# A fused attention and mixture-of-experts layer: all attention products in four column tiles, and four pieces of work moved by a step or a unit

## What is computed

```python
logits = jnp.einsum('bhnd,bhmd->bhnm', Q, K) * scale        # Q, K rotated
logits = jnp.where(causal, logits, -jnp.inf)
attn = einsum('bhnm,bhmd->bhnd', softmax(logits), V) @ Wo.T
x = layernorm(x + attn)
xf = layernorm(x, ln_w, ln_b)
router = xf @ router_w;  top = argmax(router);  score = sigmoid(max(router))
shared = (silu(xf @ sh_gate) * (xf @ sh_up)) @ sh_down
xe = xf * score of its own expert e
routed = (silu(xe @ gate_w[e]) * (xe @ up_w[e])) @ down_w[e]
out = layernorm(x + (x + routed + shared))
```

## Time and profile before

| | |
|---|---|
| median of 3 runs | 934.19 us (933.56 to 934.78) |
| the profiled execution | 932.65 us |
| its span | 930.9 us |
| TensorE busy | 904.8 us, 97% of the span |
| VectorE busy | 730.3 us, 78% |
| ScalarE busy | 469.6 us, 50% |
| GpSimd busy | 387.4 us, 42% |

### The profile page before, as it was taken

How to read it: one execution, slowest core, us unless ns; L and a number is a source line. 1 busy time by engine, 2 the same in 40 slices (tenths; PEclk the granted TensorE clock), 3 DMA queues, 4 the chain that set the end, 5 groups by cost and what they waited for, 6 DMA issues and landing times. The chain is left out here.

```text
span 930.9 us, 23459 instructions
## 1 busy us (share of the span) xinstructions
PE 904.8 (97%) x8215; PEld 570.3 (61%) x8215; DVE 730.3 (78%) x1813; ACT 469.6 (50%) x655; POOL 387.4 (42%) x521
## 2 busy tenths in 40 slices
PE   9999899999999999999999889999999999999996
PEld 5556444444444444444434268888887999848996
DVE  5889899999999999999977657777777467575554
ACT  2454377777776777777656732222223232373321
POOL 8996232332233333323333421444446233333344
PEclk9999999999999999999999999999999999999999
DMA  8798344566665475856631186433345232223321
GB/s 315 187 252 241 55 64 64 59 82 87 105 82 93 58 108 62 126 76 82 142 42 13 13 244 210 144 90 93 92 144 177 78 95 75 68 65 86 82 71 41
DMA packets 174832, 99.25 MB, mean 107 GB/s; under 512 B 132480, under 2 KB 161408, under 8 KB 171520
## 3 DMA queue, kind: packets, MB, share of 16 engines
q1 hardware_dynamic: 161344, 71.85, 40.6%
q0 software_dynamic: 4800, 13.38, 3.9%
q10 hardware_dynamic: 8576, 12.58, 3.9%
HBM read 65.05 MB, written 32.31 MB: 105 GB/s over the span
## 5 line engine op out<-in xcount | busy, mean ns | idle before, releaser
L1160 ACT ACTIVATE probs<-scores_ps 128x1024 f32<-128x1024 f32 (+3 forms) x384 | 289.8, 810 | 96.4 <-PE scores_ps L1101 95.9
L320 DVE TENSOR_REDUCE maxima<-max_ps 128x1 f32<-128x512 f32 (+2 forms) x352 | 224.3, 680 | 28.6 <-PE max_ps L278 15.2
L278 PE MATMUL max_ps<-k_stack,q_stack 96*32 96x512 bf16 (+5 forms) x1731 | 224.5, 347 | 4.7 <-DMA q_stack<-q_parts 2.0
L1241 POOL TENSOR_SCALAR_AFFINE_SELECT probs<-probs 128x512 f32<-128x512 f32 x128 | 81.8, 639 | 261.7 <-ACT probs L1160 261.5
L1101 PE MATMUL scores_ps<-q_stack,k_stack 99*32 99x512 bf16 (+5 forms) x1824 | 186.3, 352 | 3.0 <-ACT probs L1160 1.4
L1121 PE MATMUL out_ps<-probs,v_ones 128*32 128x512 f32 (+3 forms) x1536 | 161.6, 493 | 3.9 <-POOL probs L1241 3.2
L315 DVE CUSTOM_DVE_ANT_0 masked_out<-max_ps,mask_wide 128x384 bf16<-128x384 f32 (+1 forms) x256 | 150.5, 617 | 7.1 <-PE max_ps L278 4.2
L278 PEld LDWEIGHTS max_ps<-k_stack,q_stack 96*32 96x32 bf16 (+1 forms) x1731 | 78.4, 95 | 107.1 <-DVE maxima L320 36.4
L1639 ACT ACTIVATE silu<-gate_ps 128x512 f32<-128x512 f32 x68 | 40.7, 598 | 184.1 <-PE gate_ps L1540 112.0
L1101 PEld LDWEIGHTS scores_ps<-q_stack,k_stack 99*32 99x32 bf16 (+1 forms) x1824 | 69.2, 97 | 92.7 <-ACT probs L1160 30.5
L2012 POOL DMA_INDIRECT out<-out_t,target_i x36 | 45.1, 1252 | 88.6 <-DVE out_t L1941 88.6
(11 more groups left out here) (221 smaller groups left out, 1342.5 us busy)
## 6 DMA issues: line engine op xcount, KB each, us to landing
k_stack<-k_parts SPq DMA_DIRECT2D x96, 128.0 KB, 4.3
q_stack<-q_parts SPq DMA_DIRECT2D x96, 128.0 KB, 7.3
q_parts<-parts SPq DMA_DIRECT2D x32, 192.0 KB, 3.2
k_parts<-parts SPq DMA_DIRECT2D x32, 192.0 KB, 3.3
sums_in<-expert_sums SPq DMA_DIRECT2D x31, 136.0 KB, 2.1
heads_rows<-heads_out SPq DMA_DIRECT2D x128, 32.0 KB, 2.1
res<-in_x SPq DMA_DIRECT2D x8, 512.0 KB, 6.2
heads_in<-heads_rows SPq DMA_DIRECT2D x64, 64.0 KB, 4.1
```

What stands on the lines that cost most here:

```text
L278: last = nc.tensor.matmul(part[a:b], self.q_stack[:ROWS, u.slot, h0 + k, t * P + a:t * P + b], self.k_stack[:ROWS, u.slot, h0 + k, chunk * ...
L320: nc.vector.tensor_reduce(self.maxima[:, u.slot, chunk, h0:h0 + heads, t], self.bank("piece", u.i, n)[:, :heads * keys].rearrange("p (h k) ...
L1160: nc.scalar.activation(probs[:, s % RING, 2 * pair:2 * pair + 2, n0:], scores_ps[:, pair, :, n0:], ACT.Exp).then_inc(exp_done, 1)
L1241: nc.gpsimd.affine_select(out=tile, in_=tile, compare_op=ALU.is_ge, fill=0.0, base=0, pattern=[[0, GROUP], [1, P]], channel_multiplier=-1) ...
```

## The change

It does five things. (1) Every score, piece and mask product of `attend` is done in four quarters; `project` still calls `find_max` whole, and `turn_max` stays as it is. (2) `fill_tails` goes from unit 12 to unit 13. (3) The first `times_wo` goes from steps 9 and 10 of unit 14 to steps 10 and 11. (4) `turn_heads` of block 1 goes from the head of `feed` into `attend` (unit 15, step 9), and in `feed` the `times_wo` of block 1 stands ahead of `gate(0, 0)` and no longer behind `up(0, 0)`; `norm_first` is cut in two, so that in block 0 `times_up(0, 1)` stands between its halves. (5) VectorE does `add_shared(i, 2)` ahead of `leave_xf_low`; `count_ranks` of block 7 goes behind `gate(7, 0)`; in block 7 `times_up(7, 2)` goes behind the tables.

```diff
-    TILED = {*range(3 * 3 + 2, 3 * 7), *range(3 * 9 + 2, 3 * 12), 0}
...
-    def find_max(self, pe, u, which, place=None):
+    def find_max(self, pe, u, which, tiles=WHOLE):
...
-                for a, b in self.column_tiles(place) if heads == 1 else WHOLE:
+                for a, b in tiles:
                     last = nc.tensor.matmul(part[a:b], self.q_stack[:ROWS, u.slot, h0 + k, t * P + a:t * P + b],
...
                 if diagonal:
-                    last = nc.tensor.matmul(part[:, keys - P:], self.ident_bf[:], self.mask[:],
-                                            start=False, stop=True)
+                    for a, b in tiles:
+                        last = nc.tensor.matmul(part[a:b, keys - P:], self.ident_bf[:, a:b], self.mask[:],
+                                                start=False, stop=True)
...
-    OPEN = {"turn_heads": (UNITS - 2, 8), "times_wo": (UNITS - 2, 9), "norm": (UNITS - 1, 0), "scale": (UNITS - 1, 3),
+    OPEN = {"turn_heads": (UNITS - 2, 8), "times_wo": (UNITS - 2, 10), "norm": (UNITS - 1, 0), "scale": (UNITS - 1, 3),
...
-                if u.i == GROUPS + 8:
+                if u.i == GROUPS + 9:
                     f.fill_tails(sp)
...
-                    for a, b in m.column_tiles(3 * s + pair):
+                    for a, b in QUARTERS:
                         last = nc.tensor.matmul(scores_ps[a:b, pair, k, n0:],
...
                     if (u.i, s) == OPEN["norm"]:
                         f.norm_first(dve, 0, 0, 0)
+                        f.second_moments(dve, 0, 0, 0)
...
                         f.choose(dve, 0, 0, 0)
+                        f.turn_heads(dve, 1, 0, 1)
...
+                if opening:
+                    front(f.times_wo)
                 for n in range(IC):
                     gate(i, n, odd)
+                    if nxt is None and n == 0:
+                        f.count_ranks(pe, i, batch, odd)
                     up(i, n, odd)
-                    if opening and n == 0:
-                        front(f.times_wo)
...
-                front(f.count_ranks)
+                if after is not None:
+                    front(f.count_ranks)
...
                 front(f.norm_first)
+                opening = isinstance(i, int) and i == 0
+                if opening:
+                    times_up(i, 1)
+                front(f.second_moments)
                 if behind:
                     f.find_place(dve, i, batch, odd)
-                if nxt is not None:
+                if nxt is not None and not opening:
                     times_up(i, 1)
                 front(f.scale_second)
-                times_up(i, 2)
+                if nxt is not None:
+                    times_up(i, 2)
                 times_up(i, 3)
...
+                add_shared(i, 2, odd, batch)
                 if nxt is not None:
                     f.leave_xf_low(dve, dve_stood, nc.vector.tensor_tensor, i + 1, nxt, 1 - odd)
-                add_shared(i, 2, odd, batch)
...
+                    times_up(2 * batch + 1, 2)
                     copy_up(0)
...
-            f.turn_heads(dve, 1, 0, 1)
```

More of the change, by code:

```diff
@@ L257, in bank_free @@
             pe.wait_ge(self.normed, 2 * u + n + 1)
-    def column_tiles(self, place):
-        return QUARTERS if place in self.TILED else WHOLE
-    def find_max(self, pe, u, which, place=None):
+    def find_max(self, pe, u, which, tiles=WHOLE):
         if not u.exists():
@@ L896, in norm_first, with second_moments @@
         self.link(dve, i, last)
+    def second_moments(self, dve, i, batch, odd):
         self.take_moments(dve, i, self.x1[:, odd])
@@ L1135, in step @@
                     score(u, s, 0)
-                    m.find_max(pe, ahead, places[3 * s], 3 * s)
+                    m.find_max(pe, ahead, places[3 * s], QUARTERS)
                     if s == 9:
@@ L1139, in step @@
                     score(u, s, 1)
-                    m.find_max(pe, ahead, places[3 * s + 1], 3 * s + 1)
+                    m.find_max(pe, ahead, places[3 * s + 1], QUARTERS)
                     if (u.i, s) == OPEN["times_wo"]:
@@ L1145, in step @@
                     times_v(behind, (s - 1) % STEPS)
-                    m.find_max(pe, ahead, places[3 * s + 2], 3 * s + 2)
+                    m.find_max(pe, ahead, places[3 * s + 2], QUARTERS)
             pe.wait_ge(m.k_ones, 1)
@@ L1584, in expert_down, with block_step @@
                 last.then_inc(down_done, 1)
-            def block_step(i, odd, nxt, after):
+            def block_step(i, odd, batch, nxt, after):
                 def front(part):
@@ L1622, in step @@
                 after = None if last else batch + 1
-                block_step(2 * batch, 0, batch, after)
-                block_step(2 * batch + 1, 1, after, after)
+                block_step(2 * batch, 0, batch, batch, after)
+                block_step(2 * batch + 1, 1, batch, after, after)
             pe.wait_ge(f.split_step, f.SPLITS_MADE)
```

## The result

The changed kernel takes 940.12 us (median of 5 runs, 935.91 to 941.23); the kernel before, on the same chip, 934.19 us (933.02 to 935.08). The ratio is 1.0059, with a 95% interval of 1.0036 to 1.0083: slower by 0.6%, a small loss but clear of the spread, where 914.6 us was forecast, and outside the range. The profiled execution took 935.91 us, the shortest of the five, for a span of 934.2 us; that of before had 930.9.

A forecast was written before the change was run, and what follows sets the result against it. TensorE, busy 97% of the span, bounds the kernel, with VectorE right behind in part of each unit; 11.8 + 1.4 + 3.4 + 0.4 + 1.3 + 1.3 = 19.6 us off 932.65 gives 913.05, as median 914.6 us (905 to 925).

The forecast's parts named there:

- Slower: the supply of products: Rival, chance 0.04: an inner attend unit's 545 products at 54 ns each take 29.4 us; kernel at about 966 us.
- Quarters everywhere: attend units 0 to 13: fewer switches between whole and quarter products save 0.84 us each, 11.8 us (5.6 to 19.3).
- VectorE did not take more than I gave it: Rival, chance 0.14: VectorE in attend lets only 0.4 us a unit through; 920.8 us (918 to 926).
- Narrow quarters are dear: Rival, chance 0.12: in attend, four quarters of 128 columns cost 0.10 us, not 0.06; 934.7 us.
- Tails: Unit 13: unit 15's query stack load, issued ahead of the tails, removes a wait and low clock; 3.4 us (1.7 to 3.5).
- Units 14 and 15: Last two attend units: quarters save 0.7 us each, 1.4 us, with ScalarE's exponentials binding.
- `times_wo`: Unit 14: first times_wo one step later saves 0.4 us of the 0.97 us wait for heads_t (0 to 1).
- Block 0: Block 0: an earlier norm saves 1.3 us (0 to 1.8); the wait moves from up(0, 3) to down(0, 0).
- Blocks 6 and 7: add_shared ahead of leave_xf_low removes the 1.60 us wait at down(6, 3); 1.3 us saved (1.0 to 1.8).
- a stack lands late in another unit: Sign in attend that would show the prediction wrong; no size given.

The follow-up runs named there:

- paced_more: paced_after with the heads_in loads split over two units each and, in block 0, VectorE's last two times_up moved ahead of scale_second; 913.99 us.
- others_alone: The changed kernel with the quarters put back to the kernel before's table of slots, the other edits kept; 929.11 us.
- before_longer_burst: The kernel before with six more 128 KB transfers, into unused stack partitions, behind each unit's twelve stack loads; 974.01 us.
- paced_after: The changed kernel with each unit's twelve stack loads issued in six pairs, one pair a step, instead of one burst; 919.31 us.

## Why the prediction was wrong

**The step that failed** is the rival "Slower: the supply of products". I asked only how fast the sequencer hands products on, found at most 17 ns each at the head of `feed`, and gave the supply 0.04. That part holds: 47 ns a product run without a stall. What I left out is that instructions come by DMA, in the same engines as the stacks, and that the rate which matters is blocks of 256 against the longest time for which one waits behind a burst. Both could be had from the profile before: the instruction queue's row on its page, a DMA share at its full value at the head of a unit (columns as in the earlier trace rows), and 545 products in place of 343:

```profile
q8 instruction: 64, 1.05, 0.5%
...
217.00:222.00 5.00, 5.00 (x53) 2.42 (x55) 4.33 (x8) 3.28 (x7) 1.48 (x3) 1.00 1.04 136
222.00:227.00 5.00, 5.00 (x92) 2.48 (x88) 4.97 (x14) 4.40 (x6) 1.22 (x2) 1.00 1.06 132
```

The cost was 22.0 us of the 22.9 by which the profiled execution (935.91) missed my 913.05.

**The other terms**, with `paced_more`'s or `others_alone`'s units where the stalls hide them in the changed kernel:

- *Quarters everywhere*, 11.8: units 0 to 13 took 375.97 us before and take 360.46 in `paced_more`, 15.51 less; 3.48 of it is unit 13's tails, so 12.0. An inner unit saves 0.81 against 0.84; the total is above 14 times that because unit 0 saves 1.1 and unit 8, with its late block before, 1.2. Right, and VectorE did not take more than I gave it.
- *Narrow quarters are dear*: fell. Eight groups of four quarters of 128 columns start 0.05 to 0.06 us apart, the whole row of them in 0.46 us (400.85 to 401.31), and nothing of the 25 ns shows between column tiles:

```profile
400.85 0.24 PE L273 MATMUL max_ps<-k_stack,q_stack 96*32 96x128 bf16 x4
400.90 0.24 PE L278 MATMUL max_ps<-mask,ident_bf 128*32 128x128 bf16 x4
400.96 0.24 PE L273 MATMUL max_ps<-k_stack,q_stack 96*32 96x128 bf16 x4
...
401.26 0.24 PE L278 MATMUL max_ps<-mask,ident_bf 128*32 128x128 bf16 x4
401.31 0.61 PE L1119 MATMUL out_ps<-probs,v_ones 128*32 128x256 f32 x8
```

- *Tails*, 3.4: 3.48 (30.06 to 26.58 in `others_alone`). Right, with the lower clock in it.
- *Units 14 and 15*, 1.4, and *`times_wo`*, 0.4: together 0.3 us (51.16 to 50.83 us from the first `times_v` of unit 14 to the last of all). Too much: ScalarE's exponentials end the waits there. The 0.97 us for `heads_t` went, and 0.56 and 0.20 us for the exponentials came in its place, so that unit 14 lasts 28.35 us in `others_alone` against 28.41.
- *Block 0*, 1.3: from the last `times_v` to the first `gate` of block 1 32.3 us before and 30.9 after, 1.4. Right, and so is where the wait went, to `down(0, 0)`, 1.85 us instead of some 1.6:

```profile
563.61 1.30 PE L1503 MATMUL down_ps<-sh_down_sb,shared_t 128*128 128x256 f32 x4 [1.85 <-DVE shared_t L1738]
```

- *Blocks 6 and 7*, 1.3: 0.9, a little under its low bound. The 1.60 us at `down(6, 3)` is gone; in its place TensorE waits 0.63 us in `down(7, 0)` for the last `shared_t`, which VectorE starts at 725.33, behind the tables of block 7 and a copy for the expert slots:

```profile
726.06 0.70 PE L1503 MATMUL down_ps<-sh_down_sb,shared_t 128*128 128x256 f32 x2 [0.63 <-DVE shared_t L1738]
```

Blocks 1 to 5 gave 0.3 that I hadn't claimed, and the start 0.2. The sum of what was gained is 18.8 against 19.6. The last line of the prediction names "a stack lands late in another unit" as a way to be wrong; it was not the stack that landed late but what stood behind it.

Left open: why the changed kernel's executions differ by 5 us and those of before by 2. Where a block boundary falls in the burst decides a stall's length, and a shift of a microsecond would change that; no run here shows it.

## What to carry to other kernels

Before cutting instructions into smaller ones, count instructions per microsecond as blocks of 256, and lay the block's duration beside the longest burst of transfers that it may have to wait behind: the page's instruction queue and the DMA share by windows give both. Idle time "by issue" in the middle of a group of products, at the same remainder of 256 each time, is a late block, and behind those of 2.2 us and more the clock was lower too (0.94 over units 4 and 6, 0.89 over unit 8). The better cure here was at the DMA queue (918 to 919 us) and not at the engine (922 us with whole products in the burst): issue a unit's loads in portions gated by the unit's steps, and look at what the same queue carries behind them. A short gap doesn't always show among the waits: products overlap in the timeline, so compare the units' lengths too.

## What was not expected of the hardware

- A packet of instructions can start 7.0 us (10.1 us with the longer burst) after the block ahead of it is entered, while 1.5 MB of stack loads stand in the data queue. The Trainium skill ("DMA: Bandwidth & Descriptors", Queues, rings and completion order) says that a DMA engine takes the queues in turn and drains a whole packet, typically of some 9 to 17 descriptors, from one before it switches. The delay agrees with that more than with a switch after each transfer of 8 KB; no run here measures the turn itself.
- A block of instructions was first executed 1.3 to 1.7 us after its packet had landed, in the stalls of the changed kernel and of `before_longer_burst`.
- Stalls of 1.1 and 1.5 us (units 0 and 2) left the granted clock at 1.00; behind one of 2.3 us it was 0.66 over five microseconds. A wait of 1.84 us in block 0 of `paced_after` was followed by 0.52 over 3.5 us, and one of 1.85 us at the same place of the changed kernel by 1.00 (564.5 to 568 us).
- The same bytes as a copy within HBM and as a load into sixteen partitions differ in how long they hold the DMA engines: 3.0 points of share more than before against 9.7, and the second is of a longer span. As share times span that is 27 us against 112.
